# A graph attention kernel: the weighing of eight gathered rows is split between two engines

## The reference

```python
xs = (x @ W_src).reshape(N, HEADS, HID)
a_src = jnp.einsum('nhc,hc->nh', xs, att_src)
a_dst = jnp.einsum('nhc,hc->nh', xd, att_dst)
e = jax.nn.leaky_relu(a_src[src] + a_dst[dst], NEG_SLOPE)
m = jax.ops.segment_max(e, dst, num_segments=N)
ee = jnp.exp(e - m[dst])
alpha = ee / (segment_sum(ee, dst)[dst] + 1e-16)
out = jax.ops.segment_sum(xs[src] * alpha[:, :, None], dst)
```

## Time and profile before

| | us |
|---|---|
| median of 3 runs (lowest, highest) | 11416.79 (11414.73, 11421.61) |
| the profiled execution's own time | 11442.35 |
| its span in the trace | 11440.6 |
| the attention stage's groups in the span | about 9753 to 11370 |

### The profile page before, as it was taken

The page is one execution under the profiler, slowest core; times in us unless marked ns, Lnnn a source line. Parts: engine busy times, 40 slices in busy tenths (PEclk is TensorE's granted clock), DMA queues, the critical chain, the costliest instruction groups (busy, mean ns, idle before and its releaser), DMA issues. The chain is left out here.

```text
span 11440.6 us, 101276 instructions
## 1 busy us (share of the span) xinstructions
PE 6292.7 (55%) x23034; PEld 4223.4 (37%) x23034; DVE 5511.1 (48%) x14364; ACT 2818.6 (25%) x9436; POOL 6474.5 (57%) x7265
## 2 busy tenths in 40 slices
PE   0656635444566664666656665555544445566664
PEld 0333323333444442333433333222233334555554
DVE  9206046666544454444644446333343234566666
ACT  0323235555322222111211112000010002444444
POOL 0666646565566645666466663666666665444443
PEclk9999976666677776777877777666665555676666
DMA  6111123333211123333233332333321112111112
GB/s 232 49 48 48 49 70 87 84 85 83 45 45 45 44 36 90 89 89 89 65 91 88 89 89 65 92 90 90 91 51 46 46 46 40 36 35 35 34 34 32
DMA packets 344419, 770.72 MB, mean 67 GB/s; under 512 B 121029, under 2 KB 175577, under 8 KB 337226
## 3 DMA queue, kind: packets, MB, share of 16 engines
q0 software_dynamic: 251328, 600.99, 20.7%
q1 hardware_dynamic: 85066, 105.97, 3.1%
q10 hardware_dynamic: 7488, 57.94, 1.3%
HBM read 616.04 MB, written 148.41 MB: 67 GB/s over the span
## 5 line engine op out<-in xcount | busy, mean ns | idle before, releaser
L580 DVE TENSOR_TENSOR acc<-acc,ps 128x256 f32 (+3 forms) x4992 | 1878.6, 376 | 3798.7 <-remote 1989.6
L929 PE MATMUL ps<-rows,hot 128*128 128x256 f32 (+2 forms) x5824 | 1868.0, 450 | 2074.4 <-issue 1189.7
L764 POOL DMA_INDIRECT rows<-table_gcn,index_dst x2080 | 1979.0, 951 | 1137.7 <-issue 581.9
L929 PEld LDWEIGHTS ps<-rows,hot 128*128 128x128 f32 x5824 | 1279.1, 261 | 2692.8 <-issue 1708.5
L810 ACT ACTIVATE ut<-u,fld 128x128 f16<-128x128 f16 x1664 | 576.7, 393 | 3188.1 <-DVE u L854 2328.5
L764 POOL DMA_INDIRECT rows<-table_gat,index_dst x832 | 785.4, 944 | 837.2 <-DVE pay L2001 586.9
L499 POOL DMA_INDIRECT dst_rows<-pay,acc x782 | 766.0, 980 | 703.1 <-ACT pay L483 462.0
L764 POOL DMA_INDIRECT rows<-table_lin,index_dst x832 | 785.3, 944 | 620.0 <-ACT index_dst L624 320.6
L741 PE MATMUL ps<-prod,hot 128*128 128x257 f32 x1664 | 658.0, 552 | 722.7 <-DVE prod L706 326.9
L764 POOL DMA_INDIRECT rows<-table_mean,index_src x832 | 785.7, 944 | 418.7 <-issue 232.3
L901 PE MATMUL ps<-prod,ut 128*128 128x416 f16 x3328 | 941.4, 417 | 0.0
(11 more groups left out here) (273 smaller groups left out, 9600.0 us busy)
## 6 DMA issues: line engine op xcount, KB each, us to landing
dst_rows<-pay ACTq DMA_DIRECT2D x52, 1088.0 KB, 31.5
fld<-dst_rows SPq DMA_DIRECT2D x104, 544.0 KB
rows<-table_gcn,index_dst POOLq DMA_INDIRECT x2080
table_gcn<-acc SPq DMA_DIRECT2D x15, 1024.0 KB
rows<-table_lin,index_dst POOLq DMA_INDIRECT x832
rows<-table_mean,index_src POOLq DMA_INDIRECT x832
rows<-table_gat,index_dst POOLq DMA_INDIRECT x832
dst_rows<-pay,acc POOLq DMA_INDIRECT x782
```

The costliest lines, as they stand in the source:

```text
L580: c.nc.vector.tensor_tensor(to, to, product, ALU.add).then_inc(c.added.sem, 1)
L764: pool.indirect_dma_start(to(q, j), None, table, bass.IndirectOffsetOnAxis(ap=c.idx[k][:, t:t + 1], axis=0)).then_inc(c.gathered[q % per]. ...
L929: pe.matmul(c.ps[:, bank(q, j), 0:used], c.hot[:, r % 2, j, :], row_of(c, s, r, j, used), start=True, stop=True).then_inc(c.mm.sem, 1)
```

## The change

The eight chunks of a group are weighed by two engines. VectorE's multiplication L2001 covers the chunks 0 to 3 alone (128x512 in place of 128x1024). ScalarE weighs the chunks 4 to 7 with eight activations (copy with a per-partition scale, 128x64 each: four chunks, two heads), placed behind the masked scores b = 3 of the next group and ahead of the copies of the turned one-hots. A new semaphore count `part` is incremented by the last of them. TensorE waits for it before the product of chunk 4, and GpSimd waits for it, beside `weighted`, before it gathers into a row buffer again.

```diff
@@ attend, ScalarE
+            def weigh(i, r):
+
+                q = RING * i + r
+                act.wait_ge(m.kept.sem, q + (m.kept.n + 1))
+                wt, rows = heads(s.wt), heads(ring_rows(c, r, width))
+                for j in range(G8 // 2, G8):
+                    for a in range(HEADS):
+                        last = nc.scalar.activation(wt[:, j, a, 0:CH], rows[:, j, a, 0:CH], ACT.Copy,
+                                                    scale=wt[:, j, a, CH:HW])
+                last.then_inc(m.part.sem, 1)
+
...
                 if nxt(i, r):
                     masked(*nxt(i, r), 3)
-
+                weigh(i, r)
+                if nxt(i, r):
                     turned(*nxt(i, r))
                     factor(*nxt(i, r))
@@ attend, GpSimd, ready(q)
                     c.hold(pool, m.weighted, m.weighted.n + q - RING + 1)
+                    c.hold(pool, m.part, m.part.n + q - RING + 1)
@@ attend, VectorE, weigh
-                nc.vector.tensor_tensor(wt[:, :, :, 0:CH], rows[:, :, :, 0:CH],
-                                        weight8.unsqueeze(3).broadcast_to([P, G8, HEADS, CH]),
+                first_half = slice(0, G8 // 2)
+                nc.vector.tensor_tensor(wt[:, first_half, :, 0:CH], rows[:, first_half, :, 0:CH],
+                                        weight8[:, first_half, :].unsqueeze(3).broadcast_to([P, G8 // 2, HEADS, CH]),
                                         ALU.mult).then_inc(m.weighted.sem, 1)
@@ attend, TensorE, product
                     before = j - 3 if j >= 3 else (-2, -1, -3)[j]
+                    if j == G8 // 2:
+                        pe.wait_ge(m.part.sem, q + (m.part.n + 1))
```

More of the change, by code:

```diff
@@ L2134, in attend @@
         x.n += 4 * NG
-    for x in (m.looked, m.scored, m.powered, m.kept, m.weighted, m.masked, m.maxed, m.factored):
+    for x in (m.looked, m.scored, m.powered, m.kept, m.part, m.weighted, m.masked, m.maxed, m.factored):
         x.n += NG
```

## The result

| | before | after |
|---|---|---|
| median of the comparison, us (lowest, highest, runs) | 11419.20 (11414.73, 11430.03, 4) | 11506.58 (11497.57, 11522.66, 4) |
| ratio after to before, 95% interval | | 1.0075 [1.0059, 1.0091] |
| span of the profiled execution | 11440.6 | 11496.9 |
| first weighing, and the hundredth after it | 9753.4, 11324.6 | 9728.6, 11380.6 |
| mean group while gathers run (100 groups) | 15.71 | 16.52 |

The change costs 0.75%, 87 us between the medians. The two spans differ by only 56 us, because the profiled execution of before entered the stage 24.8 us later than that of the change, after stages that the change does not touch. The stage itself is 80.8 us longer over the 100 groups with gathers, and 0.9 us over the last three.

A forecast was written before the change was run, and what follows sets the result against it. The gathers' release was taken to bound the loop (burst's end, look-up, scores, weighing). 8 groups at 1.73 us (14) and 92 at 0.93 (86), with the last groups 101 us, gave 11517 us; range 11460 to 11595.

The forecast's parts named there:

- What bounds the kernel: Attention stage: the end of the eight-gather burst sets the group; scores 2.60 to 2.86 us after the last gather's start.
- The sum: Attention stage: 8 groups at 1.73 us (14), 92 at 0.93 (86), with the last groups 101 us more.
- ScalarE's half: Weighing of chunks 4 to 7: eight activations, one every 0.24 us, 0.33 each, from +0.93 to +2.94.
- The gathers' release: GpSimd waits for both halves: first gather at +3.73 in place of +2.00, 1.73 us later; burst ends at +12.47.
- The copies: Turned one-hots behind ScalarE's activations: 1.92 us later, first transpose 0.87 late, last product at +8.2 to +8.7.
- Late additions fall away: VectorE's last addition mostly before +11, not +12.8; the look-up alone holds the circle, 0.93 us more than the mean group.
- The first rival: All late additions move with the burst: every group gets the full 1.73 us, 173 us, 11590; chance 0.24.
- The second rival: The delay hangs on VectorE's weighing, not the gathers: halving takes 0.55 us from 104 groups, 57 us, 11360; chance 0.09.
- Nothing moves: Activations as fast as 16-column ones: burst 0.8 us later, given back by additions, within 20 us of now; chance 0.05.

The follow-up runs named there:

- burst-in-two kernel: Kernel before, gathers five to eight of a group waiting for the last product of the group four back; ratios 0.9999, 1.0002, 1.0004 and 1.0 on chips 3, 6, 1, 9.

## Why the prediction was right

The forecast was 11517 us, 100 above the median it started from; measured are 11506.6 and 87. Step by step:

**What bounds the kernel.** Held for the ordinary groups. It rested on comparisons within one trace; the run with only the gathers moved shows it by cause: gathers 2.27 later, scores 1.56 later than the +14.30 of the earlier trace rows, and 2.8 to 2.9 behind the last gather's start in 91 of 100 groups. (In the earlier trace rows that distance is 3.56, because the late addition stands between.) Too strong was the sentence that TensorE's results become visible only when the burst has drained: in the same trace of before the addition of chunk 6 waited in 85 of the 92 other groups and always started ahead of the last gather, and with later gathers eight groups got their scores ahead of it. The sum did not use that sentence, only the distance for the look-up. A lower clock is not the cause of the long groups: six groups of the changed kernel ran at a granted clock of 0.50 throughout and took 16.5 to 16.6 us like the rest.

**ScalarE's half.** Predicted +0.93 to +2.94, measured +0.92 to +2.93. The row of another line with the same width and a pointer had the duration to the nanosecond (333), and the overlap taken from a run of four gave the rest.

**The gathers' release.** Predicted +3.73 and +12.47 for first and last; measured +3.71 (91 of 100 groups) and +12.47 (83).

**The copies.** Predicted: first transpose 0.87 late, last product done at +8.2 to +8.7, hidden behind the burst. Measured: 1.08 of idle time there, second addition at +5.05, last at +9.4 to +11. Hidden, here. The cover that the text named, the burst, is gone on the other chips: on chip 1 a group of the changed kernel takes 1.24 us more than one of the burst-in-two kernel (12.41 and 11.17), in spite of the lighter VectorE.

**Late additions fall away.** Predicted scores at +15.33 and a group of 16.64; measured +15.2 to +15.3, 16.5 to 16.6, in nearly all ordinary groups, and the last addition comes by +11.0 in 95 of the 100. The first rival (173 us) needed them to move with the burst; they came earlier by 2 to 3 us.

**The sum.** Predicted 100 us over the 100 groups, measured 81. The 84 groups that are neither long nor behind a long one gave 15.64 before and 16.59 after, 0.95 each and 80 us; the text had 0.93. The mis-sized term is the one for the groups with a late second gather, which the text made 1.73 us longer each, 14 us. Such a group of the changed kernel:

```profile
9894.68 0.68 DVE L2015 TENSOR_TENSOR pay<-rows,ps 128x512 f32<-128x512 f32 x1
...
9901.20 0.94 POOL L764 DMA_INDIRECT rows<-table_gat,index_dst  x1 [1.86 <-issue]
...
9908.41 0.18 DVE L2004 TENSOR_TENSOR pay<-rows,ps 128x16 f32<-128x16 f32 x1 [3.03 <-remote]
9908.71 0.94 POOL L764 DMA_INDIRECT rows<-table_gat,index_dst  x1 [0.30 <-issue]
9911.17 0.69 DVE L1961 TENSOR_REDUCE mx<-ps 128x4 f32<-128x512 f32 x1 [1.96 <-remote]
9911.78 0.68 DVE L2015 TENSOR_TENSOR pay<-rows,ps 128x512 f32<-128x512 f32 x1
```

The look-up came through before the burst's end (scores 0.30 ahead of the last gather), and what waited for the end was the first chunk maximum L1961, 2.46 behind the last gather's start. The scores came from 0.3 ahead of it to 1.1 behind in the eight, and L1961 in all of them 2.4 to 2.5 behind. The weighing is next behind it, at once, without the 1.31 us of the scores. Such a group took 17.09 instead of 17.94, and the one after it, in which ScalarE found its work done, 14.5 to 15.9. Together they took 32.28 on average, against 32.17 before: 1 us over eight pairs, where the sum had 21 (14 for the long ones, 7 for those behind). That is the 20 us by which it was too high. The text had read the earlier trace rows as if the same wait would stay last.

**The second rival**, that a lighter VectorE helps, and with it the rule that the prediction set beside it from the Trainium skill (SBUF — State Buffer, Who interferes with whom), by which TensorE never waits for such traffic. The run with only the gathers moved excludes the rival on chip 11: the weighing stayed, and the scores went with the gathers. In the traces of the comparison TensorE's own rows agree with the rule: the last product is shown as done, in the median group, at +7.5 before and +8.6 after. What comes late is the moment at which VectorE goes on, of which the rule says nothing; to take it for a rival of this delay went further than the rule. On chip 3 nothing waits so, and VectorE's half alone saves 0.59 us a group. That this is near the rival's 0.55 is no proof of its circle; which path the saving takes there was not followed. **Nothing moves** fell with the width of the activations, as argued.

## What to carry to other kernels

Ask of a split first what its later half releases. Here it released the gathers, and the whole loop turned about them, so that 0.5 us taken from one engine became a release 1.7 us later and a group 0.95 us longer. On an engine that takes its work in order, put first what another engine is waiting for: two copies moved ahead of eight activations made the same split a gain of 0.6% on a chip where nothing waited for the burst's end; on chip 11 that order was not tried. And a wait that is read off one group in twelve should be followed to the next wait behind it before it is multiplied.

## What the runs showed of the hardware

The kernel before takes 11.42 to 11.57 ms in the first comparison and on chip 11, and 9.58 to 9.59 ms on four other chips. In the attention stage the difference is 15.76 us a group against the 11.17 of the burst-in-two kernel on chip 1, whose whole time is that of before: 459 of the 1850 us. The rest lies ahead of it, in other stages, which have gathers too: the first weighing starts at 9739.7 on chip 11 and at 8347.5 on chip 1 in the same two traces. What holds those stages was not followed. One gather takes GpSimd the same 0.94 us on both. What in the chip makes TensorE's results show late beside a burst is not seen in any trace; nor whether the chip itself or what ran beside on it is the cause.

On chip 11 the hold is no simple gate that closes with the burst. In the trace of before, in the 92 groups without a late second gather, the addition of chunk 6 waited 85 times and started 5.7 to 8.6 us after the first gather's start, each time ahead of the last gather's. The last addition waited in all 92 and started from 0.1 ahead of the last gather's start to 2.8 behind it, 2.0 in the median. In the changed kernel the last addition waited in 88 such groups and started ahead of the last gather in 84 of them, mostly 5.7 to 7.2 us after the first gather's start. The scores, where they waited for the look-up in such groups, started 2.7 to 3.2 us behind the last gather's start in all three kernels. Where the second gather was late, they came from 5.2 ahead of the last one (gathers moved) to 2.6 behind it (before). What decides which results pass inside a burst is not shown.
